# Linear attention readout in a fused attention and FFN layer: from token-major queries and transposes to 32x32 array tiles, with reciprocal denominators spread by matmuls

## The reference

```python
def attention(x, Wq, Wk, Wv, Wp, bp, conv_w, conv_b):      # 16 heads of 16 channels
    q, k = elu(split_heads(x @ Wq.T)) + 1.0, elu(split_heads(x @ Wk.T)) + 1.0
    v = split_heads(x @ Wv.T)
    kv_state = einsum('bhnd,bhne->bhde', k, v)             # over the 1024 tokens of a batch
    k_state = k.sum(axis=2)
    attn_out = einsum('bhnd,bhde->bhne', q, kv_state)
    denom = maximum(einsum('bhnd,bhd->bhn', q, k_state), 1e-06)[..., None]
    attn_out = merge_heads(attn_out / denom)
    local = three_tap_convolution_over_tokens(x, conv_w) + conv_b
    return (attn_out + local) @ Wp.T + bp

def ffn(x, w_gate, w_up, w_down):                          # hidden size 768, weights int / 127
    return (silu(x @ wg.T) * (x @ wu.T)) @ wd.T
```

## Time and profile before

| | |
|---|---|
| median of 3 runs | 505.22 us |
| the profiled execution, its own time | 504.68 us |
| its span, first to last instruction | 503.0 us |
| TensorE busy | 490.9 us, 98% of the span |
| VectorE busy | 429.3 us, 85% |
| ScalarE busy | 332.9 us, 66% |
| GpSimd busy | 145.8 us, 29% |
| granted TensorE clock, mean | 0.999 of full |

### The profile page before, as it was taken

One profiled execution on the slowest core, in us unless ns is written; L12 is line 12 of the kernel. 1 busy time (PEld: TensorE's weight loads), 2 busy tenths in 40 slices (PEclk: granted clock), 3 DMA queues, 4 the chain that ended last, 5 costly groups with the idle time before them and its releaser, 6 DMA issues.

```text
span 503.0 us, 11007 instructions
## 1 busy us (share of the span) xinstructions
PE 490.9 (98%) x3957; PEld 305.2 (61%) x3957; DVE 429.3 (85%) x827; ACT 332.9 (66%) x522; POOL 145.8 (29%) x162
## 2 busy tenths in 40 slices
PE   7989998999999999999999999999999999999997
PEld 6545364755657475574756657475565747657576
DVE  6797998889888888888889888889988889897787
ACT  1878857667485666748577585767748567674771
POOL 4476034140501414032140502314041141401050
PEclk9999999999999999999999999999999999999999
DMA  8637332343335324252342325233342432234012
GB/s 300 192 46 166 64 106 42 86 111 56 130 44 142 69 47 132 44 155 42 100 108 42 125 42 167 42 83 106 53 133 42 129 79 42 86 50 76 3 42 85
DMA packets 68669, 45.36 MB, mean 90 GB/s; under 512 B 33440, under 2 KB 68128, under 8 KB 68640
## 3 DMA queue, kind: packets, MB, share of 16 engines
q1 hardware_dynamic: 59232, 35.66, 25.5%
q0 software_dynamic: 8448, 8.39, 11.1%
q10 hardware_dynamic: 960, 0.92, 0.5%
HBM read 20.32 MB, written 8.39 MB: 57 GB/s over the span
## 4 chain that ended last, share of the span: by engine, by line
PE 86%; DVE 8%; ACT 3%; issue 2%; POOL 0%; DVEq 0%; POOLq 0%; ACTq 0%
PE ps L1126 16%; PE ps L1285 15%; PE ps L1304 15%; PE ps L1294 14%; PE ps L1228 14%; PE ps L1184 5%; PE ps L1193 3%; PE ps L1247 2%; DVE hid L975 1%; DVE hl L981 1%; PE ps L1134 1%; DVE local L904 1%; PE ps L1169 1%; ACT hh L590 1%; DVE p_wl L745 1%
## 5 line engine op out<-in xcount | busy, mean ns | idle before, releaser
L582 ACT ACTIVATE act_g<-ps,scales 128x512 f32<-128x512 f32 x96 | 66.0, 687 | 42.0 <-PE ps L1294 40.0
L975 DVE SCALAR_TENSOR_TENSOR hid<-act_g,scales,ps 128x512 f32<-128x512 f32 x96 | 71.4, 744 | 21.3 <-ACT act_g L582 20.7
L981 DVE TENSOR_TENSOR hl<-hid,hh 128x512 f16<-128x512 f32 x96 | 66.7, 694 | 2.2 <-ACT hh L590 0.8
L365 POOL TENSOR_TENSOR xT<-xh,xl 128x1024 f32<-128x1024 f16 x15 | 31.8, 2122 | 112.5 <-issue 98.1
L590 ACT ACTIVATE hh<-hid 128x512 f16<-128x512 f32 x96 | 59.7, 622 | 5.4 <-DVE hid L975 5.4
L1285 PE MATMUL ps<-xh,g_wh 128*128 128x512 f16 x192 | 57.6, 382 | 2.1 <-DVE q_relu L930 1.2
L1294 PE MATMUL ps<-xl,g_wh 128*128 128x512 f16 x192 | 57.1, 379 | 0.0
L1294 PE MATMUL ps<-xl,u_wh 128*128 128x512 f16 x192 | 57.1, 379 | 0.0
L1285 PE MATMUL ps<-xh,u_wh 128*128 128x512 f16 x192 | 57.1, 379 | 0.0
L1304 PE MATMUL ps<-d_wh,hh 128*128 128x256 f16 x384 | 52.5, 273 | 1.3 <-DVE hid L975 1.3
L330 POOL TENSOR_SCALAR xn<-x_in,neg_mean,rstd 128x256 f32<-128x256 f32 x62 | 52.3, 857 | 4.3 <-POOL rstd L337 4.2
(11 more groups left out here) (162 smaller groups left out, 964.7 us busy)
## 6 DMA issues: line engine op xcount, KB each, us to landing
xb<-bp_sb SPq DMA_DIRECT2D x16, 512.0 KB, 3.3
xb<-in_L_attn_x_dram POOLq DMA_DIRECT2D x16, 512.0 KB, 5.9
x_in<-in_L_attn_x_dram SPq DMA_DIRECT2D x15, 512.0 KB, 4.2
out_dram<-out_sb SPq DMA_DIRECT2D x14, 512.0 KB, 2.9
wg_int<-in_L_ffn_w_gate_dram SPq DMA_DIRECT2D x1, 768.0 KB, 6.9
wu_int<-in_L_ffn_w_up_dram SPq DMA_DIRECT2D x1, 768.0 KB, 8.4
wd_int<-in_L_ffn_w_down_dram SPq DMA_DIRECT2D x1, 768.0 KB, 11.2
out_dram<-out_sb SPq DMA_DIRECT2D x3, 256.0 KB, 2.1
```

Source lines behind the costliest of these rows:

```text
L582: nc.scalar.activation(act_g[:, j % 2, :], ps[:, gate_bank(j), :], ACT.Silu, scale=silu_in).then_inc(silu_ready, 1)
L975: nc.vector.scalar_tensor_tensor(out=hid[:, j % 2, :], in0=act_g[:, j % 2, :], scalar=h_mul, in1=ps[:, gate_bank(j) + 1, :], op0=ALU.mult, ...
L981: nc.vector.tensor_tensor(hl[:, j, :], hid[:, j % 2, :], hh[:, j, :], ALU.subtract).then_inc(hl_ready, 1)
```

## The change

The readout turns round. The state is stored compactly (partition by 32 columns, for each half of the channels) and is the stationary operand, q moves, 512 tokens at a time. The output has channels on partitions, so that there is no transpose and no attn. The division is made before the product: q is multiplied by the reciprocal denominators.

- `denominators`: four f32 matmuls in 128x32 column tiles, moving 256 tokens each; stationary are the key sums (masked). They land in one PSUM bank, four groups of partitions.
- `divide_one` (VectorE): maximum with 1e-6 and reciprocal, both of 128 partitions by 256 columns.
- `spread_denominators`: four f32 matmuls in 32x128 row tiles, moving 256 columns each; stationary is a table of zeros and ones, `to_head`, that copies a head's value to its 16 channels. Four PSUM banks.
- `divide_q` (VectorE): two products of 512 columns, q by the spread reciprocals, in place.
- `numerators`: eight f32 matmuls in 32x32 tiles, moving 512 tokens each. The four row tiles of a half k write one bank, each to a group of 32 partitions of its own.
- For the second half the state's blocks are stored one partition group further on (`accumulate`), and the columns of Wq are permuted to match, by three DMAs in place of one.
- Orders: on TensorE `accumulate(0)` and `(1)` stand together between `gate_up(0)` and `gate_up(1)`, behind a wait for the divided q, and `numerators` behind `gate_up(1)`. On VectorE `relu_q` comes behind `divide_q`, the right taps behind `relu_q`, `put_y` behind `hidden_low(0)`, `put_state` at j = 3, and `put_q` between `hidden_low(4)` and `hidden_low(5)`. The last step is ordered anew.

```diff
+            def load_query_weights():
+                src = wqT.rearrange("(k p) n -> p k n", p=P)
+                for to, start, n in ((0, 0, P), (P, 2 * P - GROUP, GROUP), (P + GROUP, P, P - GROUP)):
+                    sp.dma_start(w_raw["q"][:, :, to:to + n], src[:, :, start:start + n]).then_inc(w_in["q"], 16)
...
+            nc.gpsimd.memset(to_head[:, :], 0.0).then_inc(to_head_made, 1)
...
+            for g in range(G):
+                pool.wait_ge(to_head_made, g + 1)
+                nc.gpsimd.affine_select(out=heads, in_=heads, compare_op=ALU.not_equal, fill=1.0, base=-g * GROUP,
+                                        pattern=[[-(GROUP // HPB), HPB], [0, HD]],
+                                        channel_multiplier=1).then_inc(to_head_made, 1)
...
+            def divide_one(b, c, bank):
+                dve.wait_ge(den_done, at(b, c, 1, 1))
...
+                nc.vector.tensor_scalar(den[:, :], ps[:, bank, 0:DEN_TOKENS], 1e-6, None, ALU.max).then_inc(den_kept, 1)
...
+                nc.vector.reciprocal(rden[:, c, :], den[:, :]).then_inc(den_inv, 1)
+
+            def divide_q(b, c):
+                dve.wait_ge(den_spread, at(b, c, 1, 1))
+                for k in range(KT):
+                    here = q_sb[:, c, k, :].rearrange("p (h t) -> p h t", h=2)
+                    ins = nc.vector.tensor_tensor(here, here, ps[:, SPREAD + 2 * k:SPREAD + 2 * k + 2, 0:DEN_TOKENS],
+                                                  ALU.mult)
+                ins.then_inc(q_divided, 1)
...
                 if attend:
-                    normalise(b - 1, c, 0, QKV)
-                    normalise(b - 1, c, 1, QKV)
+                    divide_one(b - 1, c, DEN)
                     put_k(0)
-                tap(pb, pc, 0, 2)
-                tap(pb, pc, 1, 2)
+                    put_k(1)
+                    divide_q(b - 1, c)
...
                     relu_q()
-                    put_y(b - 1, c, 0, TURNED)
-                    put_y(b - 1, c, 1, TURNED)
+                    tap(pb, pc, 0, 2)
+                    tap(pb, pc, 1, 2)
                 if ahead:
                     for j in range(J):
                         hidden(j)
-                        if j == 0 and attend:
-                            put_q(b, c)
...
                         if j >= 1:
                             hidden_low(j - 1)
+                        if j == 1 and attend:
+                            put_y(b - 1, c, 0, NUM)
+                            put_y(b - 1, c, 1, NUM)
+                        if j == 3:
+                            put_state()
+                        if j == 5 and attend:
+                            put_q(b, c)
...
                     hidden_low(J - 1)
-                    put_state()
...
@@ VectorE, last step (replaces the order there)
+                    hidden(0)
+                    put_state()
+                    hidden(1)
+                    hidden_low(0)
+                    put_y(b - 1, c, 0, NUM)
+                    put_y(b - 1, c, 1, NUM)
+                    hidden(2)
+                    hidden_low(1)
+                    put_q(b, c)
+                    divide_one(b, 0, LAST_DEN[0])
+                    y_low(b - 1, c, 0)
+                    hidden(3)
+                    hidden_low(2)
+                    y_low(b - 1, c, 1)
+                    hidden(4)
+                    hidden_low(3)
+                    divide_q(b, 0)
+                    hidden(5)
...
@@ TensorE
+            def denominators(b, c, bank):
+                pe.wait_ge(state_ready, b + 1)
+                pe.wait_ge(q_ready, at(b, c, 1, 1))
+                for k in range(KT):
+                    for h in range(2):
+                        g = (2 * k + h) * GROUP
+                        ins = nc.tensor.matmul(ps[g:g + GROUP, bank, 0:DEN_TOKENS], key_sums[:, side_of(b), k, :],
+                                               q_sb[:, c, k, h * DEN_TOKENS:(h + 1) * DEN_TOKENS], start=True, stop=True,
+                                               tile_position=(0, g))
+                ins.then_inc(den_done, 1)
+
+            def spread_denominators(b, c):
+                pe.wait_ge(den_inv, at(b, c, 1, 1))
+                pe.sem_inc(num_due, 1)
+                for g in range(G):
+                    rows = slice(g * GROUP, (g + 1) * GROUP)
+                    ins = nc.tensor.matmul(ps[:, SPREAD + g, 0:DEN_TOKENS], to_head[rows, :], rden[rows, c, :],
+                                           start=True, stop=True, tile_position=(g * GROUP, 0))
+                ins.then_inc(den_spread, 1)
+
+            def numerators(b, c, banks):
+                pe.wait_ge(q_divided, at(b, c, 1, 1))
+                pe.sem_inc(num_due, 1)
+                for k in range(KT):
+                    for r in range(G):
+                        rows, g = slice(r * GROUP, (r + 1) * GROUP), (r - k) % G * GROUP
+                        ins = nc.tensor.matmul(ps[g:g + GROUP, banks[k], :], state[rows, side_of(b), k, :], q_sb[rows, c, k, :],
+                                               start=True, stop=True, tile_position=(r * GROUP, g))
+                ins.then_inc(num_done, 1)
...
                 if attend:
                     pe.wait_ge(res_ready, at(b, c - 1, 2, 2))
-                    pe.wait_ge(acc_kept, at(b, c, 1, 0))
-                    query(b - 1, c, 0, QKV)
-                    query(b - 1, c, 1, QKV)
+                    denominators(b - 1, c, DEN)
                 project_kv(1)
                 project_q()
+                if attend:
+                    spread_denominators(b - 1, c)
+                gate_up(0)
+                if attend:
+                    pe.wait_ge(q_divided, at(b - 1, c, 1, 1))
                 accumulate(0)
+                accumulate(1)
+                gate_up(1)
                 if attend:
-                    transpose_attn(b - 1, c, 0, TURNED)
-                    transpose_attn(b - 1, c, 1, TURNED)
-                accumulate(1)
-                gate_up(0)
-                gate_up(1)
+                    numerators(b - 1, c, NUM)
...
@@ TensorE, last step (replaces the order there)
+                    gate_up(2)
+                    denominators(b, 0, LAST_DEN[0])
+                    gate_up(3)
+                    gate_up(4)
+                    pe.wait_ge(y_ready, at(b - 1, c, 2, 2))
+                    spread_denominators(b, 0)
+                    gate_up(5)
+                    pe.wait_ge(q_divided, at(b, 0, 1, 1))
+                    denominators(b, 1, LAST_DEN[1])
+                    project_y(b - 1, c, 0, WP)
+                    project_y(b - 1, c, 1, WP)
+                    pe.wait_ge(hid_ready, at(b, c, J, J - 1))
+                    numerators(b, 0, LAST_NUM[0])
+                    pe.wait_ge(hid_ready, at(b, c, J, J))
+                    down(0, LAST_DOWN)
+                    pe.wait_ge(out_ready, at(b - 1, c, 2, 2))
+                    spread_denominators(b, 1)
+                    pe.wait_ge(y_ready, at(b, 0, 2, 2))
+                    project_y(b, 0, 0, LAST_WP[0])
+                    project_y(b, 0, 1, LAST_WP[0])
+                    numerators(b, 1, LAST_NUM[1])
+                    down(1, LAST_DOWN)
+                    project_y(b, 1, 0, LAST_WP[1])
+                    project_y(b, 1, 1, LAST_WP[1])
```

More of the change, by code:

```diff
@@ L59, in at, with side_of @@
         return b * (CB * per_step) + (c * per_step + k)
+    def side_of(b):
+        return 1 if isinstance(b, int) and b == NB - 1 else 0
     with ExitStack() as ctx:
@@ L136, in build @@
         whole_acc = sb("whole_acc", [P, KT, VW])
-        state = sb("state", [P, KT, AW])
-        den = sb("den", [P, 2, 2, KT, HPB])
-        rden = sb("rden", [P, 2, 2, KT, HPB])
-        attn = sb("attn", [P, TILES, D])
-        first_q_relu = attn[:, :, :].rearrange("p (k i) d -> p k (i d)", k=KT)
+        state = sb("state", [P, 2, KT, GROUP])
+        key_sums = sb("key_sums", [P, 2, KT, GROUP])
+        den = sb("den", [P, DEN_TOKENS])
+        rden = sb("rden", [P, CB, DEN_TOKENS])
+        to_head = sb("to_head", [P, P])
+        first_q_relu = sb("first_q_relu", [P, KT, CHUNK])
         local = sb("local", [P, KT, S])
@@ L158, in build @@
         STATE = 6
[L159 to L160 removed]
+        DEN = 7
+        NUM = [4, 5]
         MAX_BANK = [7, STATE, 7]
@@ L867, in put_y @@
                     dve.wait_ge(wp_done, at(b, c, 2, p - 1))
-                nc.vector.scalar_tensor_tensor(out=y[:, :, cols], in0=halves(banks[p]), scalar=attn_to_y,
+                both = ps[:, banks[0]:banks[1] + 1, cols]
+                nc.vector.scalar_tensor_tensor(out=y[:, :, cols], in0=both, scalar=attn_to_y,
                                                in1=local[:, :, c * CHUNK + p * PAIR:c * CHUNK + (p + 1) * PAIR],
@@ L1051, in step @@
                         hidden(j)
-                        if j == 0 and attend:
-                            put_q(b, c)
-                        elif j == 0:
+                        if j == 0 and not attend:
```

(42 more changed lines are left out.)

108 lines of the change are left out of this document (36 added, 72 removed).

## The result

The changed kernel takes 512.88 us (median of 4 runs, 511.10 to 513.40), the kernel before 505.2 us beside it: ratio 1.0144, 95% interval 1.0131 to 1.0157, so 7.7 us slower. The forecast was 510.0 us. The profiled execution took 512.68 us with a span of 511.1 us, against 503.0 us before: 8.1 us more.

The account below looks back on a forecast made before the run. TensorE was taken to bound the kernel, plus what VectorE makes it wait. Full steps +1.7, last step +3.1 and start +0.5 sum to +5.3 us: 510.0 us, the forecast's own range 503 to 517, overall 498 to 526.

Parts of the forecast that it names:

- TensorE's work, -0.42 us a step: Full step: query -1.85 and accumulates with transposes -1.12 saved, denominators, spread and numerators +2.55 added with tiling changes.
- The stall at hl, +0.35: End of a full step: hidden_low(5) now stands behind put_q, so TensorE waits 0.35 us with the semaphore.
- The wait for q_relu, +0.2: Full step: gate_up(1) on TensorE waits 0.2 us for relu_q, which VectorE runs behind the divided q.
- The step's sum, +0.13: A full step: TensorE's work -0.42, hl stall +0.35, relu_q wait +0.2; taken 13 times, +1.7 us.
- divide_one covered in a full step, uncovered in the last: VectorE's reciprocal 1.75 us and maximum 0.43: done at 6.8 before the spread at 8.4, but delaying TensorE in the last step.
- The start, +0.5: Kernel start: two more DMA issues on SyncE before the gate weights, 0 to +1.0 us, taken as +0.5.
- The last step, +3.1: Last step: TensorE's list 39.7 us, waits 4.9 and 1.1 to the last output, 45.7 against 42.6 us.
- (A): Rival: small tiles stream in half the time, 498 us; chance 0.25 together with hidden changes of tiling.
- (C): Rival: two tiles on one strip of 32 rows don't stream together, numerators take two rounds, 522 us; chance 0.08.
- (B): Rival: the spread's full-width f32 weight loads come one by one, spread 0.95 us or more, 516 us; chance 0.10.
- (D): Rival: program order makes one tile per record time, +4.15 us a readout, 572 us; chance 0.07.
- (E): Rival: one row tile at a time into a bank, so numerators run one by one, 600 us; chance 0.02.

Follow-up runs that it names:

- experiment 1: Changed kernel with q_sb's sum issued after the last hl, not between hid(5) and hl(5), in the look-ahead steps: 506.49 us, ratio to before 1.0029.
- experiment 6: Changed kernel with the reciprocal of the denominators replaced by a multiplication and addition of constants: 509.55 us, ratio 1.0081.
- experiment 2: Changed kernel with q_sb's sum of (0,1) issued between the two k_sb sums in step (1,0): 509.22 us, ratio 1.0115.
- experiment 3: Changed kernel with the state's sums in step (0,1) issued after the last hl, not after hid(3): 512.35 us, ratio 1.0146.
- experiment 7: Kernel of experiment 4 with the eight 32x32 products of the numerators issued twice: 517.04 us, ratio 1.0222.
- experiment 8: Kernel of experiment 4 with the four row-tile products that spread the denominators issued twice: 508.86 us, ratio 1.0084.
- experiment 4: Changed kernel with the edits of experiment 1, experiment 2 and experiment 3 together: 502.69 us, ratio 0.9950.
- experiment 5: Kernel of experiment 4 with the last step reordered on VectorE and TensorE: 503.28 us, ratio 0.9955.
- experiment 9: Kernel of experiment 5 with GpSimd's four additions of outer taps cut from 512 to 16 columns: 500.23 us, ratio 0.9905.
- experiment 10: Kernel of experiment 5 with GpSimd's two subtractions for yl ahead of its four additions, nothing left out: 500.48 us, ratio 0.9904.

## Why the prediction was right, point by point

Slower it was, by 7.7 us where 4.8 were forecast, inside the forecast's own range (503 to 517). The prices, the stall at hl and the last step came out by their mechanism. 3.2 of the 8.1 us are in two steps for which the sum has 0.13; that the total stayed in the range in spite of them is owed to its width.

- **TensorE's work, -0.42 us a step: right**, -0.41. Denominators 0.57 + 0.11 = 0.68 (0.65 forecast), spread 0.75 (0.75), numerators 1.02 + 0.11 = 1.13 (1.15).
- **The stall at hl, +0.35: right in place, too small.** It is 0.50 in the mean (experiment 1). In the steps (b,0) it is 0.37, as forecast. In the steps (b,1) it is the 0.62 read above: there `put_state` at j = 3 puts the sums for the state ahead of hid and hl, and the chain runs through them. The sum had them at nothing. (No run moves them alone in a full step.)
- **The wait for q_relu, +0.2: there, and smaller**, 0.14. It stays in experiment 1.
- **"30.00 us without a gap": misread.** The step read is one of the six (b,0); the six (b,1) take 29.83. In a (b,0) step `gate_up(2)` waits 0.17 us for hid, from 263.66 to 263.83, and each step has 0.06 more at `gate_up(3)`:

```profile
263.23 0.59 PE L1294 MATMUL ps<-xl,u_wh 128*128 128x512 f16 x2
263.83 0.60 PE L1285 MATMUL ps<-xh,g_wh 128*128 128x512 f16 x2
...
263.83 0.11 PEld L1285 LDWEIGHTS ps<-xh,g_wh 128*128 128x128 f16 x2 [0.49 <-DVE hid L975]
```

- **The step's sum, +0.13: measured +0.10, partly by luck.** It is -0.41 for TensorE's work, +0.14 for q_relu, +0.50 for hl, and -0.14 for the old kernel's own waits, which are gone in experiment 1. The forecast had nothing for the last of these and 0.15 us too little for the stall at hl, and the two cancel. So the 0.40 us between 29.50 and 29.90 equal TensorE's saving only because q_relu's wait came and the old waits went.
- **divide_one covered in a full step, uncovered in the last: right.** The reciprocal takes 1.753 us, the maximum 0.42 (0.43 forecast); experiment 6 shows both halves.
- **The first step with a readout: the step that failed.** The forecast said "13 times ((1,0) to (7,0))" and took (1,0) as one of the full steps, +0.13 us; it got +2.25. `put_q(0, 1)` stands there, and only there, ahead of relu_q. Moved behind the divided q it makes ScalarE's q_neg wait 3.45 us and TensorE 2.5 us, and in this execution the clock fell behind that pause, for 1.4 us more (experiment 2). The kernel before was 1.5 us over its normal step here too (31.52 for 29.99), so the difference is 2.25 and not 3.9.
- **Step (0,1) was left out of the sum**, +1.0 us. `put_state` at j = 3 also moves in the step without readout, with the group_mask reduction, ahead of hid and hl (experiment 3).
- **The start, +0.5: too large**, +0.1. VectorE's wait for the gate weights is 0.5 us for 0.32.
- **The last step, +3.1: right**, +3.5. TensorE's waits were forecast as 1.5 (spread, L1224), 0.6 (`gate_up(5)`, L1325), 1.9 (denominators, L1213) and 0.7 (project_y, L1155). The view of waits from 462 us on (us in total, times, longest):

```profile
PE ps L1213 <- DVE q_sb L874: 2.6, 1, 2.6
PE ps L1224 <- issue: 1.4, 1, 1.4
PE ps L1155 <- POOL yl L498: 0.6, 1, 0.6
PE ps L1325 <- DVE hid L997: 0.4, 1, 0.4
```

The spread's wait has no releaser in this view ("issue"), but it ends at 484.67, 0.10 us behind the end of the reciprocal, which the code waits for. The divided q came later than forecast because the hl ahead of it took 1.55 us beside GpSimd's additions, for 0.68. A second one, 1.14 us at 490.88, stands behind the divided q and ahead of the second reciprocal.

- **The rivals.** (A), half price, and (C), two rounds, fall with the numerators' 1.02 and experiment 7's 0.86 a set. (B), (D) and (E) fall with experiments 7 and 8: a second set of row tiles costs 0.43, and four row tiles that write one bank, each its own partitions, run together. The sentence that the Trainium skill (TensorE: Matmul & The Clock Gate, Part 3) has on program order does not keep tiles from overlapping here; its page TensorEngine Tiling (Array Packing), Restrictions and Gotchas, says that different row tiles cannot use one PSUM bank at the same time. `numerators` does so at the price of one pass, and the measurement decides.

## What to carry to other kernels

A cheaper product pays only if the order of the engine that feeds it is kept: here 0.41 us a step were won on TensorE and 0.50 lost by one sum ahead of the wrong operation on VectorE. With the order mended the same products made the kernel 2.6 us faster than before (experiment 4). When an operation is moved in a generator, walk through every step that has it, the ones that occur once too: two such steps made 3.2 of the 8.1 us. A forecast that takes one repeated step times its number missed exactly these.

## What was unexpected of the hardware

- VectorE's operations with both operands in SBUF took up to 2.3 times as long while GpSimd added in SBUF (q_sb 2.29 us for 1.22, hl 1.10 to 1.55 for 0.68), and those with one operand in PSUM kept 0.73. The Trainium skill (SBUF — State Buffer, Who interferes with whom) says that a VectorE instruction with two SBUF inputs contends with a GpSimd instruction that reads SBUF; the traces of experiments 5, 9 and 10 agree. Not every overlap shows it: in experiment 10 an hl that began at 482.88 kept 0.68 us, though GpSimd's subtraction began at 483.04.
- A pause of TensorE of 2.5 to 2.6 us was followed by half the clock in some profiled executions and by the full clock in others. In step (1,0) of the changed kernel the granted clock was 0.50 from 83.2 to 86 us, and in experiment 1, whose order is the same up to there, it stayed at 1.00. In the last step it stayed at 1.00 in experiment 4 and was 0.83 from 490 to 500 us in experiment 7.
